# Clamp and Newton step of the local norms on GpSimd instead of VectorE, with new merge orders of the streams

## The reference, cut to what matters

```python
# x: [8, 512, 128]; six modulation vectors per batch from silu(c) @ wmod
h = layernorm(x) * (1 + ca) + sa
x = x + ga * attention16(h)              # 16 heads of 8 features, over features
h = layernorm(x) * (1 + cb) + sb
x = x + gb * ffn(h)

# ffn: two layers; in each, with 8 heads of 64 and windows of 64 tokens
h = shift_token(x)
q, k, v = split(h @ wqkv)
q = q / max(norm(q), 1e-12) * q_scale    # per head: the local norms
k = k / max(norm(k), 1e-12) * k_scale
q, k = rotary_xpos(q, k)
x = x + local_attention(q, k, v) @ wo
h = layernorm(shift_token(x)) * lg + lb
a, g = split(h @ w1 + b1)
x = x + (a * gelu(g)) @ w2 + b2
```

## Time and profile before

| | |
|---|---|
| median of 3 runs | 1196.69 us (1193.58 to 1197.32) |
| the profiled execution | 1196.15 us, its span 1194.3 us |
| PE busy | 997.0 us, 83% |
| DVE busy | 949.4 us, 79% |
| ACT busy | 918.2 us, 77% |
| POOL busy | 508.1 us, 43% |
| mean granted TensorE clock | 0.948 of full speed |

### The profile page before, as it was taken

How to read it: one execution, slowest core, us unless ns; L and a number is a source line. 1 busy time by engine, 2 the same in 40 slices (tenths; PEclk the granted TensorE clock), 3 DMA queues, 4 the chain that set the end, 5 groups by cost and what they waited for, 6 DMA issues and landing times. The chain is left out here.

```text
span 1194.3 us, 23996 instructions
## 1 busy us (share of the span) xinstructions
PE 997.0 (83%) x8124; PEld 510.0 (43%) x8124; DVE 949.4 (79%) x1947; ACT 918.2 (77%) x2782; POOL 508.1 (43%) x578
## 2 busy tenths in 40 slices
...
DMA packets 28009, 59.18 MB, mean 50 GB/s; under 512 B 6192, under 2 KB 6384, under 8 KB 26736
## 3 DMA queue, kind: packets, MB, share of 16 engines
...
...
## 5 line engine op out<-in xcount | busy, mean ns | idle before, releaser
L905 ACT ACTIVATE E<-psum,neg_max 128x512 f32<-128x512 f32 x512 | 346.6, 716 | 64.2 <-DVE neg_max L1191 45.9
L1191 DVE TENSOR_REDUCE neg_max<-psum 128x2 f32<-128x1024 f32 x256 | 307.5, 1214 | 58.7 <-PE psum L465 56.7
L465 PE MATMUL psum<-v_rows,k_rows 64*128 64x512 f32 x512 | 130.3, 514 | 106.0 <-ACT E L905 79.6
L998 ACT ACTIVATE rot_work<-psum,neg 128x128 f32<-128x128 f32 x512 | 184.3, 412 | 17.9 <-DVE neg L1284 11.0
L838 POOL TENSOR_TENSOR rot_work<-rot_work,rz 128x512 f32<-128x512 f32 x128 | 133.0, 1047 | 141.0 <-DVE rz L1289 140.9
L825 POOL TENSOR_TENSOR work<-work,rot_work 128x512 f32<-128x512 f32 x96 | 121.7, 1273 | 129.6 <-DVE rot_work L1262 129.3
L465 PEld LDWEIGHTS psum<-v_rows,k_rows 64*128 64x128 f32 x512 | 52.8, 196 | 250.6 <-ACT E L905 116.1
L803 POOL TENSOR_TENSOR qz<-qT,rz 128x32 f32<-128x32 f32 x128 | 30.8, 241 | 300.7 <-DVE rz L1195 299.8
L523 PE MATMUL psum<-wqkv_sb,hs 128*128 128x512 f32 x288 | 144.0, 622 | 6.8 <-DVE hs L1248 3.8
L474 PE MATMUL psum<-E,qz 128*32 128x512 f32 x1024 | 148.2, 653 | 0.2 <-POOL qz L803 0.2
L998 ACT ACTIVATION_READ_ACCUMULATOR rot_work<-psum,neg 128x1 f32 x512 | 126.7, 252 | 0.0
...
## 6 DMA issues: line engine op xcount, KB each, us to landing
k_rows<-k_scr SPq DMA_DIRECT2D x128, 64.0 KB, 1.9
...
v_rows<-v_scr SPq DMA_DIRECT2D x124, 64.0 KB, 1.9
...
```

Source lines behind the costliest of these rows:

```text
L465: pe.matmul(bank, k_rows[r:r + 64, half, hh, P * j:P * (j + 1)], v_rows[r:r + 64, b % 2, hh, :], start=True, stop=True).then_inc(full, 1)
L905: act.activation(E[:, (b * NG + g) % E_RING, 2 * half + m, :], pair[:, m], ACT.Exp, bias=neg_max[:, n, m:m + 1], accum_out=z[:, n, m:m + 1 ...
L998: last = act.activation(pr[s][:, u % PR_SLOTS, w, :], bank[:, 2 * W * w:2 * W * (w + 1)], ACT.Exp, bias=neg2[s][:, u, w:w + 1], accum_out= ...
L1191: dve.tensor_reduce(neg_max[:, n, :], pair, AX.X, ALU.max, negate=True).then_inc(max_ready, 1)
```

## The change

The clamp and the Newton step move from VectorE's `b_stream` to GpSimd's. The clamp becomes a `tensor_scalar` with two immediates, so the constant tile `clamp` goes, with the memset and the semaphore for it. The Newton step becomes four GpSimd instructions instead of three of VectorE, chained by semaphore waits on `rn_chain`. Logarithm and exponential stay on ScalarE at the same places of its stream. The strings of `ORDER` for all five engines and `BANKS` are new.

```diff
-B_CHAIN = LN_CHAIN + (2 * 2 + LN_CHAIN) * L
+B_CHAIN = LN_CHAIN + LN_CHAIN * L
...
-        clamp = sb("clamp", [P, J, H])
...
-            pool.memset(clamp[:], SHIFT2).then_inc(s_clamp, 1)
...
+            def b_norm(s, k, l, w):
+                passed(pool, ss_ready[s], (k * L + l) * 2 * J + J * (2 - w))
+                v = ss[s][:, :, w, :]
+                pool.tensor_scalar(v, v, NORM_MIN2, SHIFT2, ALU.max, ALU.mult).then_inc(ss_all[s], 1)
+
+            def b_rnorm(s, k, l, w):
+                n = (k * L + l) * 2 + 1 - w
+                pool.wait_ge(ss_rsqrt[s], n + 1)
+                v, r, t = (a[s][:, :, w, :] for a in (ss, rn, nt))
+                pool.tensor_tensor(t, v, r, ALU.mult).then_inc(rn_chain[s], 1)
+                pool.wait_ge(rn_chain[s], 4 * n + 1)
+                pool.tensor_tensor(t, t, r, ALU.mult).then_inc(rn_chain[s], 1)
+                pool.wait_ge(rn_chain[s], 4 * n + 2)
+                pool.tensor_scalar(t, t, -0.5, 1.5, ALU.mult, ALU.add).then_inc(rn_chain[s], 1)
+                pool.wait_ge(rn_chain[s], 4 * n + 3)
+                pool.tensor_tensor(r, r, t, ALU.mult).then_inc(rn_chain[s], 1)
...
             def b_scale(s, k, l, i, w):
                 if i == 0:
-                    pool.wait_ge(rn_ready[s], (k * L + l) * 2 + 2 - w)
+                    pool.wait_ge(rn_chain[s], 4 * ((k * L + l) * 2 + 2 - w))
...
                             b_rotary(s, k, l, n)
                             yield
+                            if n == J - 1:
+                                b_norm(s, k, l, 1)
+                                yield
+                            if n == J:
+                                b_rnorm(s, k, l, 1)
+                                yield
...
+                        b_norm(s, k, l, 0)
+                        yield
+                        b_rnorm(s, k, l, 0)
+                        yield
                         for i in range(J):
                             b_scale(s, k, l, i, 0)
...
-            def b_norm(s, k, l, w):
-                passed(dve, ss_ready[s], (k * L + l) * 2 * J + J * (2 - w))
-                v = ss[s][:, :, w, :]
-                dve.scalar_tensor_tensor(v, v, NORM_MIN2, clamp[:], ALU.max, ALU.mult).then_inc(ss_all[s], 1)
-
-            def b_rnorm(s, k, l, w):
-                dve.wait_ge(ss_rsqrt[s], (k * L + l) * 2 + 2 - w)
-                newton(ss[s][:, :, w, :], rn[s][:, :, w, :], nt[s][:, :, w, :], b_link_of(s, k)).then_inc(rn_ready[s], 1)
```

More of the change, by code:

```diff
@@ new lines @@
+        "xaaxaaaaaxaaxxxxxxxaaxxaxaaaaaaaxxaaaaxxxxaaaaaaaaaaaxaaxxaaaxaaaxxaaaxxxxaxxaaaaaxaxxaaxaxaaaxxaaax"
+        "aaxaaaaaaxaaaaaaxaxxxxxxaaaxaaaaaaxxxxxaaxaxxaaxaxaaaaaaaxaxaxxxxaaaaaxxaxxxxyxxxxxyxxyxxyxyyxyxyxyx"
+        "yxyxyyyxyxxxxxxyxyxyyyyyyxzxxxxxxxxxzxzzzzzxxzxxxxzzzyyyyyxxxxxxyyzxzxzxxxzzzxxxyxyxyxxzzzzxzxzxzzzx"
+        "zyyzyzzxyxzxzzxxxzxyzxzyzxzxxxzyxxxyyyyyyxzxyxzyzzzyyyzzyxxzyyxxzzzxzyzzyyzzzzxxxxxxxyyyyyyxxxxxxxxx"
+        "xzzxxyyyzzyxyyzxzxyzyyxzzzyyyyxzxyxyyxxyxxzzxzxzyyzzyzzxyzzzxyxxxxxxxxxyzzyyyyyyyzyxzxxxzxyxyyyzyyyy"
@@ L83 @@
+        "yyyxxxxxxzyyzzzzzyyyyxzzxxzxxyyyyxxyzyxxxzzzzzzzzzzyyyxxxyyyyzzxzzzzyyxyyyxyzyzyzzxyzzxxxxxzzxyzxzzz"
+        "zxxzzzxxxzxxzzxzxxzyyzxyyyyxyzxxzzyyyyyyyxyyyzzzzxxzxxxzzzzzzzzzzyxxyyyzzyyzzzzxxxxxxxzzxxzzzzxyyyyx"
+        "xxyzzxzxzzzzxyzzyyzyxyyxzxxxyxxyzzyyxzyzyyyzxyyzyzzzzzzyzyyzyyyyyy"
     ),
@@ new lines @@
+        "axaaaaaxxaxxaaxxxxxaxxaaxaxaxxxaxaaaaaxxxxxaaaaaxaxaxxxaxaaxxaxaxxaxxxaaaxaaaaaxaaaxaaaxaxaaaaaaaxaa"
+        "axaxaxaxaxaaxxxxxxxxaxaaaaxaaaxaaxxxaxaxaaaxaxxaaxaaaxxxaaxxxxaxxxaaaxaxxaaxaxxaaaaxaaaaxaaxaaxaaaxa"
+        "axaxxxaxxaxxaxaxxaaaaxaxxaxxaxxaaxxxxyxxxyxxxyxxyxxyxxyxxyyyxyxyyxyyxyyyxyxyyyyyyxyzxxzyzxyxyxxxxxxx"
+        "zxxzzzzxzxzxxxzxxzyyzyyxxxxyzyxxxzxxxzzyyxzxxxzxzxzxxyyxzzyzzxzzzzxzzzxyzyxzzzzxzzyzzxyxxzxxyxxzxyxz"
+        "xyxxyzyyyyxxyzyxxzzzxzxyzzyyyzzzzxxxxxxxxyyyxxxzyyxxxxxyxyxxzzxyyyzzyxyzzzyyyxzyyyxzzzyxyyyzzyxyzzzz"
```

99 lines of the change are left out of this document (37 added, 62 removed).

## The result

The changed kernel takes 1198.18 us (median of 20, 1194.29 to 1203.63), the kernel before on the same chip 1195.41 us (20 runs, 1191.32 to 1198.19). The ratio is 1.0024, 95% interval 1.0013 to 1.0034: slower by a quarter of a per cent, which is less than the 0.3% that the forecast calls no change. The forecast said 1180 us, and its own range ended at 1193.

What follows compares the result with a forecast made beforehand. ScalarE and VectorE were taken to set the pace beside a, no engine with two streams, TensorE with three. 561.8 + 24 + 62 + 530 = 1177.8 us of span, plus 1.9, gave 1180 us; own range 1162 to 1193, overall 1158 to 1206.

Steps and rivals of the forecast that it cites:

- the one beside a: Stretch where streams a and x share the core: +24 us, between ScalarE's +30 and VectorE's +19; a ends at 585.8 us.
- loses the six norm sets that lay beside a, 6 x 1.79 = 10.7 us: While a and x run: VectorE is relieved of six norm sets at 1.79 us busy each.
- GpSimd's price: Norm sets on GpSimd: five instructions and three waits, 1.5 us a set, 48 us in all.
- take nothing, with bounds of -10 us and +22 us: Last stretch, 22 norm sets: shorter sets on GpSimd against their queueing behind its additions, net zero.
- Two streams: Stretch after a ends where only x and y run: 62 us, 59 less than 121; TensorE's work 50 us.
- the bound of 68.8 us by x's chain: Stretch of x and y: x's way from transposed queries to result bounds its length by 68.8 us.
- Three streams: Last stretch, from z's begin: TensorE's work 485 us at a fill of 0.916, 530 us, 18 more than 511.5.
- TensorE is the limit: Last stretch, all three streams: TensorE sets the time, busy for 468.5 of 511.5 us (0.916).
- The second: Rival: ScalarE alone sets a's stretch (+30 us), x's chain the stretch of two; 1192.5 to 1195.7 us, no change, chance 0.14.
- The first: Rival: GpSimd stands still within norm sets and holds other streams, 1 us a set; 1212 us, slower, chance 0.20.
- one of its signs: Signs of the slower rival: a ends after 600 us, with long `nt` waits for ScalarE and TensorE waits for `qz`.
- The third: Rival: ScalarE's 26 us more fit into its idle time beside a, which ends at 561.8 us; 1156 us, chance 0.10.

Runs made afterwards that it cites:

- e3: The kernel before (old order) with clamp and Newton step left out of every norm set: 1176.74 us, ratio 0.9838 to the kernel before.
- e4: The changed kernel (new order) with clamp and Newton step left out of every norm set: 1188.69 us, ratio 0.9927 to the kernel before.
- e12: The changed kernel itself, unchanged, run and profiled a second time: 1198.16 us.
- e13: e3 with one more half-width maximum on VectorE before every fourth maximum of stream a: ratio 0.9998 to the kernel before.
- e14: e3 with four more TensorE products of 256 columns in 7 of 16 groups of stream a: ratio 0.9896 to the kernel before.
- e15: e3 with one more ScalarE copy of 256 columns before every fourth pair of stream a's exponentials: ratio 0.9940 to the kernel before.
- e9: e4 with every fourth VectorE maximum of stream a taken over half of its columns: ratio 0.9909 to the kernel before.
- e2: The kernel before, with its old order and banks, but clamp and Newton step made by GpSimd: 1199.88 us, ratio 1.0034 to the kernel before.
- e7: The changed kernel with the clamp folded into the logarithm, so GpSimd makes the Newton step alone: 1191.32 us, ratio 0.9964 to the kernel before.

## Why the prediction was wrong

Against the median-like second profile the forecast span of 1177.8 us is 18.5 us short: +14.0 beside a (599.8 for 585.8), -3.2 with two streams (58.8 for 62), +7.7 with three (537.7 for 530).

**The step that failed** is the one beside a: "loses the six norm sets that lay beside a, 6 x 1.79 = 10.7 us", and with it the middle "+24 us". Two things are wrong in it. The relief of 10.7 us isn't there: leaving the sets out altogether brings a's end from 561.8 to 560.4 (e3). And the stretch was priced as if VectorE or ScalarE alone set it, so that relief of one and load of the other could be balanced between them. The runs put in its place: -1.4 us for the sets gone from VectorE (e3), +32.7 for the order (e4 against e3), +6.7 for the sets on GpSimd (e12 against e4), +38.0 in all for the +24. Each is a difference of single profiles, good to a few us. e13 to e15 show that load on any of the three engines costs some 0.4 to 0.6 of itself, TensorE's too, which the forecast left out beside a, and e9 that relief of one returns about a seventh. The counts of the moved work were right: VectorE's added work was put at 26.6 us and measured 25.7 (e4 against e3), TensorE's at 33 and measured 34.8, ScalarE's at 26 and measured 21.0. VectorE's 26.6 without the credit, over its fill, would have been +32, and the measured order without sets is +32.7. That agreement is luck: by e13's rate VectorE's load would cost 14 us of it. How the three loads make up the 32.7 stays open, as no run added x's steps alone.

**GpSimd's price**: 1.5 us a set, measured 1.31 busy and some 0.25 between the instructions of the chain, right. Its effect: "take nothing, with bounds of -10 us and +22 us" for the last stretch. In the old order, e2 against before, it is +3.0 us (514.5 to 511.5), within the bounds, and +3.1 with two streams. What the step did not have is that the clamp holds ScalarE (8.3 us beside a), and that e7 wins back 7 us by taking the clamp away.

**Two streams**: forecast 62, measured 58.8; TensorE's work 50, measured 47.6. Right, and the bound of 68.8 us by x's chain did not hold.

**Three streams**: TensorE's work 485, measured 488.0, at a fill of 0.908 where 0.916 was taken; 3 us by work and 5 by fill. The sets cost 4.7 us there (537.7 to 533.0 without them). "TensorE is the limit" is also weaker than it read: in the old order the sets, that TensorE has no part in, cost this stretch 14.5 us (511.5 to 497.0).

**The rivals.** The second, that what x gains a pays, is what happened in effect: it gave 1192.5 to 1195.7 us, and the time is 1198.2. Its mechanism, ScalarE alone, is not what the runs show. The first, GpSimd holding the others, showed one of its signs (a at 602.6 and 599.8 us) without the long waits: beside a `nt` waits 1.7 us for ScalarE, and TensorE 4.3 us for `qz` (3.5 in e4). All of GpSimd's sets cost 9.5 to 11.6 us, 0.3 to 0.4 us each and not the 1 us at which it stood. The third is excluded. The chance of 0.14 for no change was too low, since a gain of 16.5 us was to come from a forecast whose one term beside a could be off by as much.

The rule of the Trainium skill that the forecast weighed ("Perfetto Trace Analysis", section "Optimizing Scalar/DVE Operations") came out on the right side here: the offload from VectorE to GpSimd brought nothing (e2, 1.0034). Its reason, the shared port, is not what e2 shows: there the sets' blocking on VectorE is gone (in the last stretch it is busy for 377.8 us, 375.5 in e3 without any sets), and TensorE's waits for GpSimd took its place (56.1 us of them there, 40.6 in the kernel before).
